# Two experts per block of rows in a mixture-of-experts kernel, and one operation for a block's low half

## What is computed

```
x = x + gnn(layernorm(x), adj)
x = x + ffn(layernorm(x))

def gnn(x, adj):
    h = layer_norm(x, gamma, beta)
    agg = einsum('bij,bjh->bih', adj, h)
    conv = agg @ W_rel + b_rel + h @ W_root
    return x + relu(conv)

def ffn(x):                       # E = 8 experts, 2 of them for each row, D = 128, H = 512
    scores = x @ Wg.T + bg
    topk_scores, topk_idx = top_k(scores, 2)
    combine = softmax(topk_scores) put at topk_idx
    for e in range(E):
        h = relu(x @ W1[e].T + b1[e])
        out = out + combine[..., e] * (h @ W2[e].T + b2[e])
    return out
```

## Time and profile before

| | |
|---|---|
| median of 3 runs | 480.88 us (479.68 to 481.05) |
| the profiled execution | 481.32 us, span 479.5 us |
| TensorE matmul, weight load | busy 393.0 us (82%), 350.2 us (73%) |
| VectorE, ScalarE, GpSimd | 315.6 us (66%), 271.5 us (57%), 249.9 us (52%) |
| TensorE's granted clock, mean | 0.936 of 2.4 GHz |
| the chain that ended last | TensorE 57%, VectorE 22%, ScalarE 7%, "issue" 6%, DMA 3%, GpSimd 3% |

### The profile page before, as it was taken

The page is one execution under the profiler, slowest core; times in us unless marked ns, Lnnn a source line. Parts: engine busy times, 40 slices in busy tenths (PEclk is TensorE's granted clock), DMA queues, the critical chain, the costliest instruction groups (busy, mean ns, idle before and its releaser), DMA issues.

```text
span 479.5 us, 13216 instructions
## 1 busy us (share of the span) xinstructions
PE 393.0 (82%) x4371; PEld 350.2 (73%) x4371; DVE 315.6 (66%) x1055; ACT 271.5 (57%) x572; POOL 249.9 (52%) x263
## 2 busy tenths in 40 slices
PE   2888878789998679889867999999999999999000
PEld 2873735579997568889856988889999999998000
DVE  4875764685679497756898557765478545588511
ACT  1787583557885547786634686555555555554000
POOL 3002720177710377774007777777777750777770
PEclk9998785999999799999999999999999999999755
DMA  8991740164234234633436537647567857554520
GB/s 274 389 413 69 277 98 12 40 149 112 74 83 100 68 98 109 155 94 80 66 79 172 138 102 139 142 112 162 145 153 178 202 133 121 135 156 140 175 71 33
DMA packets 100721, 65.30 MB, mean 136 GB/s; under 512 B 66866, under 2 KB 92466, under 8 KB 100020
## 3 DMA queue, kind: packets, MB, share of 16 engines
q1 hardware_dynamic: 66292, 34.68, 27.4%
q0 software_dynamic: 8192, 16.79, 12.2%
q10 hardware_dynamic: 26176, 12.98, 11.1%
HBM read 19.58 MB, written 31.85 MB: 107 GB/s over the span
## 4 chain that ended last, share of the span: by engine, by line
PE 57%; DVE 22%; ACT 7%; issue 6%; DMA 3%; POOL 3%; ACTq 0%; SPq 0%; DVEq 0%; POOLq 0%
PE PY L951 7%; PE PY L946 7%; PE PY L947 7%; PE PH L927 6%; PE PH L929 6%; PE PH L928 6%; DVE HL L521 5%; POOL YG L307 3%; PE PY L938 2%; DVE STI L361 2%; PE PB L848 2%; PE PA L856 2%; PE PA L857 2%; ACT N L670 2%; DVE STO L407 1%
## 5 line engine op out<-in xcount | busy, mean ns | idle before, releaser
L294 POOL DMA_INDIRECT rows<-XHL,IDX x128 | 124.2, 970 | 136.0 <-DVE IDX L503 97.9
L521 DVE SCALAR_TENSOR_TENSOR HL<-PH,HH 128x512 f16<-128x512 f32 x198 | 129.9, 689 | 63.6 <-ACT HH L727 61.0
L307 POOL DMA_INDIRECT YG<-yrows,IDX x128 | 121.5, 949 | 81.7 <-DMA yrows<-YB 43.6
L727 ACT ACTIVATE HH<-PH 128x512 f16<-128x512 f32 x198 | 115.4, 594 | 29.4 <-PE PH L929 24.1
L947 PE MATMUL PY<-W2H,HL 128*128 x792 | 131.8, 220 | 0.0
L946 PE MATMUL PY<-W2H,HH 128*128 x792 | 131.8, 220 | 0.0
L927 PE MATMUL PH<-XT,W1H 128*128 128x256 f16 x396 | 108.1, 273 | 2.7 <-DVE HL L521 1.7
L951 PE MATMUL PY<-W2L,HH 128*128 x792 | 109.5, 220 | 0.0
L929 PE MATMUL PH<-XT,W1L 128*128 128x256 f16 x396 | 108.0, 273 | 0.0
L928 PE MATMUL PH<-XT,W1H 128*128 128x256 f16 x396 | 107.9, 273 | 0.0
L735 ACT ACTIVATE YB<-PY 128x256 f32<-128x256 f32 x99 | 37.9, 383 | 97.4 <-PE PY L951 92.3
(11 more groups left out here) (192 smaller groups left out, 504.8 us busy)
## 6 DMA issues: line engine op xcount, KB each, us to landing
yrows<-YB ACTq DMA_DIRECT2D x47, 256.0 KB
rows<-XT SPq DMA_DIRECT2D x2, 3072.0 KB, 16.3
YG<-in_w SPq DMA_DIRECT2D x2, 2048.0 KB, 11.3
out<-X SPq DMA_DIRECT2D x16, 256.0 KB
X<-in_x SPq DMA_DIRECT2D x3, 1024.0 KB, 5.5
ADJ<-in_adj SPq DMA_DIRECT2D x32, 64.0 KB
rows<-XHL,IDX POOLq DMA_INDIRECT x128
YG<-yrows,IDX POOLq DMA_INDIRECT x128, 2.5
```

Of the source, the lines that this page charges most:

```text
L294: nc.gpsimd.indirect_dma_start(rows[g % 2], bass.IndirectOffsetOnAxis(ap=IDX[:, col:col + 1], axis=0), XHL[:, src:src + 2 * P].bitcast(F32 ...
L307: nc.gpsimd.indirect_dma_start(YG[g % 2][:, dst:dst + P], None, yrows[g], bass.IndirectOffsetOnAxis(ap=IDX[:, col:col + 1], axis=0)).then_ ...
L521: nc.vector.scalar_tensor_tensor(HL[:, at:at + 2 * BW], PH[p % 2 * 2 + h][:, :], 0.0, HH[:, at:at + 2 * BW], ALU.max, ALU.subtract).then_i ...
L727: nc.scalar.activation(HH[:, at:at + 2 * BW], PH[p % 2 * 2 + h][:, :], ACT.Relu).then_inc((hia_made, hib_made)[h], 1)
```

## The change

1. An expert's slots now begin at a multiple of 128. A block still has 256 slots, but it consists of two **parts** of 128 with an expert each. A group of s tiles needs (2 s + 8)/2 blocks: 12, 20, 20, 20 and 12, together 84.
2. TensorE loads two experts per block. The hidden part runs over both parts with 128 columns each instead of once with 256; the output part does one part after the other.
3. The two PSUM banks of a block's hidden values are one tensor, and the low half is one operation on 1024 columns, which waits for both high halves. One semaphore, `lo_made`, takes the place of two.
4. Two quads of a pair share one calculation of eight scales; the later steps of a quad follow `FINISH` instead of `START[n] + 5`.
5. The tables START, STATS, ROUTE and COMBINE have new numbers for the 84 blocks.

```diff
-NB = [s + E - 1 for s in GS]
+NB = [(2 * s + E) // 2 for s in GS]
 NP = P0[G]
...
-START = {6: 5, 7: 7, 8: 9, 9: 11, 10: 17, 11: 20, 12: 23, 13: 26, 14: 39, 15: 43}
-STATS = {2: 1, 3: 12, 4: 35}
-ROUTE = {2: 16, 3: 32, 4: 49}
-COMBINE = {0: 30, 1: 32, 2: 66, 3: 68, 4: 70, 5: 72, 6: 90, 7: 92, 8: 94, 9: 96}
+START = {6: 4, 7: 6, 8: 8, 9: 10, 10: 14, 11: 17, 12: 20, 13: 23, 14: 34, 15: 38}
+FINISH = {n: START[n | 1] + 5 + n % 2 for n in START}
+STATS = {2: 0, 3: 9, 4: 30}
+ROUTE = {2: 17, 3: 30, 4: 45}
+COMBINE = {0: 31, 1: 33, 2: 54, 3: 56, 4: 59, 5: 61, 6: 75, 7: 77, 8: 79, 9: 81}
...
-        PH = [pb(f"PH{k}") for k in range(4)]
+        PH2 = [ctx.enter_context(nc.psum_tensor(f"PH{k}", [P, 1024], F32)) for k in range(2)]
+        PH = [PH2[k // 2][:, k % 2 * 512:k % 2 * 512 + 512] for k in range(4)]
...
-                once(nc.vector.tensor_scalar(CNI[:, :], CNT[:, :], float(BW - 1), None, ALU.add))
+                once(nc.vector.tensor_scalar(CNI[:, :], CNT[:, :], float(P - 1), None, ALU.add))
-                once(nc.vector.tensor_scalar(PADI[:, :], CNI[:, :], 8, 8, ALU.logical_shift_right, ALU.logical_shift_left))
+                once(nc.vector.tensor_scalar(PADI[:, :], CNI[:, :], 7, 7, ALU.logical_shift_right, ALU.logical_shift_left))
...
-            def low_half(p, h):
-                dve.wait_ge((hia_made, hib_made)[h], p + 1)
-                at = (p % 2 * 2 + h) * 2 * BW
-                nc.vector.scalar_tensor_tensor(HL[:, at:at + 2 * BW], PH[p % 2 * 2 + h][:, :], 0.0, HH[:, at:at + 2 * BW],
-                                               ALU.max, ALU.subtract).then_inc((loa_made, lob_made)[h], 1)
+            def low_halves(p):
+                dve.wait_ge(hia_made, p + 1)
+                dve.wait_ge(hib_made, p + 1)
+                at = p % 2 * 4 * BW
+                nc.vector.scalar_tensor_tensor(HL[:, at:at + 4 * BW], PH2[p % 2][:, :], 0.0, HH[:, at:at + 4 * BW],
+                                               ALU.max, ALU.subtract).then_inc(lo_made, 1)
 
...
                 for n, at in START.items():
                     if p == at + 2:
                         residual(n)
-                    if p == at + 3:
-                        scales_out_first(n, 1)
-                    if p == at + 4:
-                        scales_out_last(n, 1)
-                low_half(p, 0)
-                low_half(p, 1)
+                for n, at in FINISH.items():
+                    if p == at - 2 and n % 2 == 0:
+                        scales_out_first(n, 2)
+                    if p == at - 1 and n % 2 == 0:
+                        scales_out_last(n, 2)
+                low_halves(p)
                 for n, at in START.items():
                     if p == at + 2:
-                        stats_out(n, 0)
-                    if p == at + 5:
+                        stats_out(n, n % 2)
+                    if p == FINISH[n]:
                         split_low(n)
                         scores(n)
                 for g, at in STATS.items():
...
-            def expert(p):
-                return nc.values_load(BEI[0:1, p:p + 1], engines=(mybir.EngineType.PE,), min_val=0, max_val=(E - 1) * P,
-                                      skip_runtime_bounds_check_because="the count of ends at or under a block is at most seven")
-
-            def hidden(p, e):
+            def experts(p):
+                return [nc.values_load(BEI[0:1, i:i + 1], engines=(mybir.EngineType.PE,), min_val=0, max_val=(E - 1) * P,
+                                       skip_runtime_bounds_check_because="the count of ends at or under a part is at most seven")
+                        for i in (2 * p, 2 * p + 1)]
+
+            def hidden(p, es):
                 ch = CB[p]
                 at = ch % XR * 2 * CW + (p - CH[ch][1]) * BW
-                hi, lo = XT[:, at:at + BW], XT[:, at + CH[ch][2] * BW:at + (CH[ch][2] + 1) * BW]
+                lo_at = at + CH[ch][2] * BW
                 if p == CH[ch][1]:
                     pe.wait_ge(xb_in[ch % XR], 16 * (ch // XR + 1))
                 for h in range(2):
-                    if p >= 2:
-                        pe.wait_ge((loa_made, lob_made)[h], p - 1)
-                    for c in (2 * h, 2 * h + 1):
-                        o = PH[p % 2 * 2 + h][:, c % 2 * BW:(c % 2 + 1) * BW]
-                        wh = W1H[:, bass.ds(e * C + c * P, P)]
-                        wl = W1L[:, bass.ds(e * C + c * P, P)]
-                        nc.tensor.matmul(o, wh, hi, start=True, stop=False)
-                        nc.tensor.matmul(o, wh, lo, start=False, stop=False)
-                        last = nc.tensor.matmul(o, wl, hi, start=False, stop=True)
+                    if p >= 2 and h == 0:
+                        pe.wait_ge(lo_made, p - 1)
+                    for t in range(2):
+                        hi, lo = XT[:, at + t * P:at + (t + 1) * P], XT[:, lo_at + t * P:lo_at + (t + 1) * P]
+                        for c in (2 * h, 2 * h + 1):
+                            o = PH[p % 2 * 2 + h][:, c % 2 * BW + t * P:c % 2 * BW + (t + 1) * P]
+                            wh = W1H[:, bass.ds(es[t] * C + c * P, P)]
+                            wl = W1L[:, bass.ds(es[t] * C + c * P, P)]
+                            nc.tensor.matmul(o, wh, hi, start=True, stop=False)
+                            nc.tensor.matmul(o, wh, lo, start=False, stop=False)
+                            last = nc.tensor.matmul(o, wl, hi, start=False, stop=True)
                     last.then_inc((ha_done, hb_done)[h], 1)
 
-            def output(p, e):
-                pe.wait_ge(loa_made, p + 1)
-                pe.wait_ge(lob_made, p + 1)
+            def output(p, es):
+                pe.wait_ge(lo_made, p + 1)
                 if p:
                     pe.wait_ge(y_made, p)
-                py = PY
-                nc.tensor.matmul(py[:, 0:BW], KH[:, H_B2M:H_B2M + P], B2[:, bass.ds(e, P)].unsqueeze(1).to_broadcast([P, 2, P]),
-                                 start=True, stop=False, skip_group_check=True)
-                for c in range(C):
-                    wh = W2H[:, bass.ds(e * C + c * P, P)]
-                    wl = W2L[:, bass.ds(e * C + c * P, P)]
-                    for t in range(2):
+                for t in range(2):
+                    o = PY[:, t * P:(t + 1) * P]
+                    nc.tensor.matmul(o, KH[:, H_B2M:H_B2M + P], B2[:, bass.ds(es[t], P)], start=True, stop=False)
+                    for c in range(C):
                         at = (p % 2 * C + c) * BW + t * P
-                        o = py[:, t * P:(t + 1) * P]
-                        nc.tensor.matmul(o, HH[:, at:at + P], wh, start=False, stop=False, skip_group_check=True)
-                        nc.tensor.matmul(o, HL[:, at:at + P], wh, start=False, stop=False, skip_group_check=True)
-                    for t in range(2):
-                        at = (p % 2 * C + c) * BW + t * P
-                        o = py[:, t * P:(t + 1) * P]
-                        last = nc.tensor.matmul(o, HH[:, at:at + P], wl, start=False, stop=c == C - 1, skip_group_check=True)
+                        wh = W2H[:, bass.ds(es[t] * C + c * P, P)]
+                        wl = W2L[:, bass.ds(es[t] * C + c * P, P)]
+                        nc.tensor.matmul(o, HH[:, at:at + P], wh, start=False, stop=False)
+                        nc.tensor.matmul(o, HL[:, at:at + P], wh, start=False, stop=False)
+                        last = nc.tensor.matmul(o, HH[:, at:at + P], wl, start=False, stop=c == C - 1)
                 last.then_inc(y_done, 1)
 
             pe.wait_ge(kf_in, 16)
...
-                e = expert(p)
+                es = experts(p)
-                hidden(p, e)
+                hidden(p, es)
-                    if p == at + 5:
+                    if p == FINISH[n]:
```

More of the change, by code:

```diff
@@ L77, in sem @@
             return ctx.enter_context(nc.semaphore(name))
-        rows = [nc.dram_tensor(f"rows{b}", [BW * (NBM + 1), P], F32, kind="Internal").ap() for b in range(2)]
+        rows = [nc.dram_tensor(f"rows{b}", [BW * NBM, P], F32, kind="Internal").ap() for b in range(2)]
         yrows = [nc.dram_tensor(f"yrows{g}", [BW * NB[g], P], F32, kind="Internal").ap() for g in range(G)]
@@ L120, in build @@
         IDX = sb("IDX", [P, 2 * TILES], I32)
-        BEF = sb("BEF", [1, NBM * (E - 1)])
-        BES = sb("BES", [1, NBM])
-        BEI = sb("BEI", [1, NP], I32)
+        BEF = sb("BEF", [1, 2 * NBM * (E - 1)])
+        BES = sb("BES", [1, 2 * NBM])
+        BEI = sb("BEI", [1, 2 * NP], I32)
         IDLE = sb("IDLE", [P, 1])
@@ L130, in build @@
         B2F, BT = HL[:, :].bitcast(F32), HH[:, 0:E * P]
-        ZW = 2 * (NBM + 1) * P // 4
+        ZW = 2 * NBM * P // 4
         ZERO = XT[:, 0:2 * ZW].bitcast(F32)
-        PH = [pb(f"PH{k}") for k in range(4)]
+        PH2 = [ctx.enter_context(nc.psum_tensor(f"PH{k}", [P, 1024], F32)) for k in range(2)]
+        PH = [PH2[k // 2][:, k % 2 * 512:k % 2 * 512 + 512] for k in range(4)]
         PY = pb("PY")
```

(16 more changed lines are left out.)

2 lines of the change are left out of this document (1 added, 1 removed).

## The result

The changed kernel takes **573.41 us** (median of four runs) against 480.61 us of the kernel before on the same chip: ratio 1.193, 95% interval 1.189 to 1.196. It is 19% slower; the prediction was 541 us. Three of the four runs took 572.24 to 573.96 us; the fourth, slow, with a mean granted clock of 0.56, took 639.24 us and is left out of the ratio.

What follows compares the result with a forecast made beforehand. The prediction took TensorE's sequencer, not its array, to bound the changed kernel: 85 us before the blocks + 411 blocks + 8 waits + 36 tail = 540 us of span, 541 us as measured time, range 508 to 578.

Steps and rivals of the forecast that it cites:

- What bounds the kernel: In the expert blocks: TensorE's sequencer, 92% full before at 2.5 us a block, becomes the bound at 4.89 against the array's 2.78.
- The prices: TensorE's sequencer: 0.115 us a register operation, 0.24 a fused and plain one together, 0.35 a load, 0.11 a wait.
- Sequencer: Expert blocks: weight addresses computed once per part make a block cost 4.89 us, 84 x 4.89 = 411 us.
- The second load: Block's head: second expert load priced at 0.35 us like the first; if wholly hidden, 29 us less.
- 84 x 4.89: Block loop: 84 blocks at two loads, eight fused-plain pairs, 18 further steps and two waits, 411 us.
- What waits remain: Sequencer waiting for ACT's copy after relations and transposes, some 0.3 us at 20 places, plus first and last block: 8 us.
- The low half: One DVE operation on 1024 columns, done some 2.3 us behind the hidden part against 4.7 us of slack: costs nothing.
- Quads' fp32 work, scales, tail: Quads' float32 matmuls, some 56 us, fit the array's spare time; shared scales gain nothing; tail unchanged at 36 us.
- The array as bound: Rival for the blocks: register steps are no price of their own, the array stays the bound, 442 us; chance 9%.
- Narrow matmuls that don't cover their loads: Rival in the hidden part: weight loads of 98 ns exposed, 3.8 us a block, 527 us; chance 2%.
- The clock: Rival in the blocks: starved TensorE's clock falls to 0.50, 692 us for good or 580 to 692 partly; chance 6%.
- Idle time that stays on top: Rival in the blocks: 29.4 us of TensorE idle time adds to the sequencer's time, 563 us and more; chance 10%.

Runs made afterwards that it cites:

- experiment 1: Changed kernel without the output part's matmul of the hidden rows' low half (8 of 50 matmuls a block), all register steps kept: 568.98 us, ratio 1.182 to the kernel before.
- experiment 2: Changed kernel with weight addresses named side by side, 10 register operations a block in place of 34, same matmuls: 489.66 us, ratio 1.016 to the kernel before.
- experiment 3: Changed kernel with one expert number loaded per block, the second part's being 7 minus the first: 554.84 us, ratio 1.152 to the kernel before.
- experiment 7: Kernel before with only the single 128x1024 low-half operation in place of two, on a slower chip: 770.11 us, ratio 1.002 to the kernel before.
- f1_grouped: The kernel of experiment 2, the changed kernel with grouped weight addresses: 489.66 us, ratio 1.016 to the kernel before.
- f4_grouped_adj: f1_grouped with quad 8's adjacency load one chunk earlier in SP's queue: 478.32 us, ratio 0.994 to the kernel before.
- i4_spread: f4_grouped_adj with the next block's loads and hidden addresses spread between output matmuls, on a slower chip: 756.89 us, ratio 0.985 to the kernel before.
- experiment 5: Changed kernel on slower chips, four separate edits: grouped addresses 759.68 us, no low-half output matmul 828.81, one load per block 822.12, earlier adjacency load 838.07.

## Why the prediction was right, and where its number was short

- **What bounds the kernel.** Right. The sequencer was 92% full in a late block before and became the bound (experiments 1 and 2).
- **The prices.** Right: 0.112 and 0.122 us a register step, 0.355 to 0.360 a load, 0.106 a wait. They gave 405.5 us for the loop where the step "Sequencer" had 411. The second load, the least sure price, was forecast at 0.35; experiment 3 took 0.28 us from a block, the load less the new step of 0.088. The Trainium skill (DMA: Bandwidth & Descriptors, Latency and other measured facts) has a floor of about 600 ns for a tensor load; the 168 loads of this trace took 302 ns in the median and disagree.
- **The term that was too small: 84 x 4.89, a block's plain prices taken for its whole time.** I read the price of a step as its usual distance and checked the sum against one block of the kernel before, 2.52 for 2.5 us. The delays between steps, 11.9 us under 0.1 us and 31.8 of 0.1 to 0.4 us in the loop before, were there in the trace, hidden under the array or counted as its waits. How many of those of 0.1 to 0.4 us were the full array holding the sequencer up isn't known. Once the sequencer is the bound such delays are on the path: 30.4 us, or 0.36 us a block. This is most of the 32 us.
- **"What waits remain", 8 us.** Mis-sized: 14.7 us, of which 6.9 are the adjacency load. I had no term for SP's queue, though the chunks at which it issues the adjacency shift with the number of blocks. The other seven long waits come to 7.8 us.
- **The low half.** Right that it costs nothing: 3.5 us of waits ahead of the output part where there were 11.2, and experiment 7. All waits of the array put down to the low half fell from 12.9 to 9.2 us and are not near nothing, but the 5.7 us among them at the head of a block lie beside the sequencer's own work.
- **Quads' fp32 work, scales, tail.** Nothing in the sequencer's count is left for them: last step at 534.9, tail 35.6 us against 36.
- **The rivals.** The array as bound (442 us): experiment 1 excludes it. Narrow matmuls that don't cover their loads: they start 0.055 us apart still where the sequencer is ahead (412.10 and 412.15 us in f1_grouped). The clock: 0.98 and 1.00. The condition given for the first rival, a register step of 0.095 us and a second load for nothing, was worked out wrongly: a block of 4.17 us follows from steps of 0.096 us with both loads paid, or of 0.106 us with one. Idle time that stays on top (563 us and more): the long waits are 14.7 and not 37 us, so the total came near that rival's by another way. That the time lies inside the range, 5 us under its upper end, is in part luck: the range had been widened for that rival and not for short delays.

Sum of the misses in the span, 570.5 - 540: -0.6 ahead of the blocks, -5.5 plain prices, +6.7 long waits, +30.4 short delays, -0.4 tail = 30.6.

What stays open: whether the change itself, freed of the sequencer, is worth anything. f4_grouped_adj is 0.6% under the kernel before; grouping alone gave the kernel before 0.9%, on a slower chip. i4_spread ran beside the grouped kernel before on one chip and is 0.7% under it (ratios to the kernel before 0.985 and 0.991), but that chip held TensorE back in both, and i4_spread has two more edits.

## What to carry to other kernels

Where weights are chosen by a register, count the sequencer's work for each block as you count the array's: so many steps by their distance, not by the 32 ns that each one shows. Splitting a block into parts with own indices multiplies that work even where the array's stays equal. Naming the addresses side by side lets them fuse, and spreading what is left between the matmuls hides a part of it. When an engine turns from hidden to bound, take its whole time with all small delays, not the sum of typical prices; and when a count of blocks changes, look through every queue for what slides behind a wait. When an experiment takes an instruction out, look in its trace for one that came in.

## What the runs showed of the hardware that was not expected

**Small delays of the sequencer.** Late in the changed kernel's loop nearly all time above the plain prices lies in single delays of 20 to 155 ns, one about every microsecond: at 467.42, 468.40, 469.58, 470.54 us (29, 154, 52 and 58 ns). They mostly come 31 or 32 recorded TensorE instructions apart, and the one of about 154 ns returns after 251 to 253 recorded ones (477.80, 487.21, 496.04 us). One of them seen from the array, in order of time; the gap of 0.21 us is in the middle of a block, where the hidden part waits for nothing:

```profile
468.50 0.22 PE L936 MATMUL PH<-XT,W1L 128*128 128x128 f16 x1
468.76 0.10 PEld L934 LDWEIGHTS PH<-XT,W1H 128*128 x1 [0.21 <-issue]
```

A fetch of instructions in pieces could look like this, but no run varied it. The Trainium skill (Runtime: NRT & Kernel Launch, Instruction fetch mechanics) says that engines refill their instructions in blocks of 256 and that the cost is mostly hidden. The period of the largest delay comes near that, but that it is the refill isn't shown. In the kernel before late blocks took the array's 2.75 us whatever the sequencer's delays; here they are on the path.

**Chips that hold TensorE back.** On two of the chips the same programs take 1.5 to 1.6 times as long (766.55 against 481.70 us for the kernel before, 828.81 against 568.98 for experiment 1's), through stretches in which matmuls come 1.4 to 2.8 us apart (experiment 5). The granted clock of such a stretch reads 0.50, which is 1.2 GHz, but a matmul every 2.8 us is far more than halving the clock explains. By the clock the first stretch begins at 109 to 118 us in all eight kernels, 15 to 22 us into the blocks. What triggers it wasn't tested.
